# Two one-word mask tiles moved, so that every small SBUF tile starts 64 bytes lower

## The chip, the core and the metric

The kernel runs on one core of one Trainium2 chip. The metric is the device time of one execution, in microseconds (us); the lower the better. A core has a tensor engine (PE, with its weight loads shown apart as PEld), a vector engine (DVE), a scalar engine (ACT), GpSimd (POOL) and a queue engine that issues the DMAs (SP). They share one on-chip memory, SBUF, of 128 partitions. A tile is a piece of it that begins at the same byte in every partition.

## What is computed

Two linear layers with low-rank adapters, each added to its own input. `x` is 8 x 256 x 1024 in float32, every weight matrix is 1024 x 1024, and the adapter of each batch is chosen by an index:

```
def layer0(x, label, W, A, Bw):          # rank 32, 3 adapters in use
    return einsum('bsi,oi->bso', x, W) + 0.5 * einsum('bsr,or->bso', einsum('bsi,bir->bsr', x, A[label]), Bw)

def layer1(x, slot, W, b, As, Bs):       # rank 16, 24 adapters in use
    return einsum('bti,oi->bto', x, W) + b + 2 * einsum('btr,bro->bto', einsum('bti,bir->btr', x, As[slot]), Bs[slot])

x = x + layer0(x, itok_B_0_2, L0_cond_W, L0_cond_lora_A, L0_cond_lora_B_w)
x = x + layer1(x, itok_B_0_23, L1_cond_W, L1_cond_b, L1_cond_lora_As, L1_cond_lora_Bs)
```

## The kernel before

The kernel first forms the product of (1 + W0) and (1 + W1) and then applies it to every batch, so that the large part of both layers is one matrix product per batch. Each float32 operand is split into a high and a low part (`_hi`, `_lo`, the type fp32r), and a product is three matmuls: high by high, high by low, low by high. Both the product of the weights and that of each batch follow a scheme of seven half-size products (names `s1` to `s4`, `t1` to `t4`, `v11`, `vt2` and so on are the sums it needs).

**Stages.** Up to about 116 us the weights are loaded, turned and multiplied; the adapters of all batches are folded into small matrices in between (`q_step` and `c_step`, from 23 to 62 us and from 84 to 90 us). Then come eight batches of about 22.7 us; six of them run in a loop. On PE a batch is: seven products of 12 matmuls with 512 columns (`product`), eight matmuls of the input with the adapter matrix (`u_product`), one small correction (`corr`), and the low-rank parts (`low_rank`, `low_rank_rest`). The order on every engine is written out by hand, and semaphores tie the engines together.

**Names in the profile.** A matmul row reads `bank<-moving,stationary`: the first name is the operand that streams through the array (here with 512, 256 or 128 columns), the second is the one that was loaded as weights by the LDWEIGHTS before it. `by_halves`, `row_product`, `vm1_high` and `product` take both operands from large tiles. `q_step` takes its weights from `b0_st`, `c_step` from `a1_st` or `a1d_hi`/`a1d_lo`, `u_product` from `ac`, `low_rank` from `u_st` (its moving operand is `p_hi`), `corr` from `b0a1` (moving `u_st`), and `low_rank_rest` moves `e_p`. The digits of the names are left out in part: `a_st`, `b_st`, `b0a`.

**The map of SBUF.** All tiles have offsets written out by hand. 23 large slots of 8192 bytes per partition (`SLOT`) lie first; the large tiles, made by `big` and a few others, are in them. Behind them lie `eye` and `blank` (512 bytes each), then `MASKS` (64 bytes, with `bias_mask` at 0 and `low_mask` at 32, one float each), and then all the other small tiles in a row: `index` at `INDEX`, `b0a1` and `b0a1_all` at `B0A1`, the tiles at `U` (`u_st`, `u_sum`, `q`, `u_part`), `p_hi`, `e_raw` and `e_p` at `P_LO`, `b1_raw`, `a1d` and `hh` at `B1_RAW`, `b0_st`, `ac` and `e_hi` at `B0_ST`, `b0_raw` and `a0_raw`, `ct`, `a1_raw`, `m1_sum`, `u2_sum` and `z_sum` at `CT`, and `a1_st`, `c_hi` and `c_lo` at `C`. Every one of these sizes except `MASKS` is a multiple of 128 bytes. The common base of all offsets, the start of free SBUF rounded up to 32, is byte 1152 in this program, 9 times 128. So the large tiles, `eye` and `blank` begin at multiples of 128, and everything from `INDEX` on begins 64 bytes past one.

Of the kernel before, what the change touches and what calls it, by code (L numbers as in the profile page):

```python
# [5 lines left out]
F32 = mybir.dt.float32  # L6
# [5 lines left out]
P = 128  # L12
# [7 lines left out]
def two_layer_lora_kernel(nc, x, label0, slot1, w0, a0, b0w, w1, bias, a1, b1, out):  # L20
# [13 lines left out]
    SLOT = HK * H * 4  # L34
    EYE = 23 * SLOT
    BLANK = EYE + P * 4
    MASKS = BLANK + P * 4
    INDEX = MASKS + 64
    B0A1 = INDEX + 256
    U = B0A1 + 1024  # L40
    P_HI = U + 3 * S * 4
# [7 lines left out]
    def at(name, shape, dt, offset):  # L49
        size = 4  # L50
        for n in shape[1:]:
            size *= n
        assert base + offset + size <= nc.sbuf_usable_end, name
        return nc.alloc_sbuf_tensor_at(name, shape, dt, offset=base + offset)
# [53 lines left out]
    blank = at("blank", [P, P], F32R, BLANK)  # L108
    index = at("index", [1, 2 * B], I32, INDEX)
    index_f = at("index_f", [1, 2 * B], F32, INDEX + 64)  # L110
    index_wrap = at("index_wrap", [1, 2 * B], F32, INDEX + 128)
    index_ok = at("index_ok", [1, 2 * B], I32, INDEX + 192)

# [28 lines left out]
    e_p = at("e_p", [P, H], F32R, P_LO + H * 4)  # L142
    e_hi = at("e_hi", [P, H], F32R, B0_ST + KT * P * 4)

    bias_mask = at("bias_mask", [P, 1], F32, MASKS)
    low_mask = at("low_mask", [P, 1], F32, MASKS + 32)
    u_part = at("u_part", [64, S], F32, U + 2 * S * 4)
    p_hi = at("p_hi", [P, D], F32R, P_HI)
    b1_raw = at("b1_raw", [P, D], F32, B1_RAW)
# [1438 lines left out]
```

## Time and profile before

| | us |
|---|---|
| median of 3 runs | 297.86 |
| lowest and highest of them | 296.70 and 298.05 |
| the profiled execution | 299.37 |
| its span, first to last instruction | 297.6 |
| PE busy | 293.0 |
| DVE busy | 242.2 |
| ACT busy | 153.2 |
| POOL busy | 29.6 |

A matmul's row has its start and its duration; matmuls overlap in the array, and so the time that one costs the engine is the distance from its start to the start of the next, its pace, and not its duration. Starts are given to 0.01 us, so a pace is best read over a stretch of many matmuls: the difference of two starts divided by the number of matmuls between them.

### The profile page before, as it was taken

How to read it: one execution, taken by the hardware profiler on the slowest of the kernel's cores; microseconds unless marked ns; L12 is line 12 of the kernel's file. 1: busy time of each engine (PE TensorE's matmuls, PEld its weight loads, DVE VectorE, ACT ScalarE, POOL GpSimd, SP SyncE). 2: the span in 40 equal slices, each digit the busy share in tenths (PEclk: the TensorE clock that was granted, in tenths of full speed). 3: DMA queues.
4: the chain of work that ended last, by engine and by line, in shares of the span. 5: the costliest groups of instructions: out<-in, count | busy, mean ns of one | idle time of the engine just before them, and what ended most of it. 6: DMA issues, size and time to landing. Idle time of an engine off the chain costs nothing.

```text
span 297.6 us, 4449 instructions
## 1 busy us (share of the span) xinstructions
PE 293.0 (98%) x1334; PEld 238.0 (80%) x1334; DVE 242.2 (81%) x368; ACT 153.2 (51%) x270; POOL 29.6 (10%) x81
## 2 busy tenths in 40 slices
PE   7999999999999999999999999999999999999996
PEld 6888888888888888877878878878878878887875
DVE  3499996999999999899997797698698698696442
ACT  3376466879355737266374364365355355355120
POOL 1717100010000501100100100100100100100000
PEclk9999999999999999999999999999999999999999
DMA  6999620620003710065168068058158149013003
GB/s 181 322 281 343 77 34 1 108 36 2 0 0 72 124 35 1 0 110 174 26 108 222 4 107 224 0 101 216 17 105 213 18 85 240 10 35 142 0 1 143
DMA packets 100803, 29.17 MB, mean 98 GB/s; under 512 B 85548, under 2 KB 93996, under 8 KB 100788
## 3 DMA queue, kind: packets, MB, share of 16 engines
q1 hardware_dynamic: 100788, 28.99, 42.1%
q8 instruction: 7, 0.11, 0.1%
q14 instruction: 8, 0.07, 0.1%
HBM read 20.59 MB, written 8.39 MB: 97 GB/s over the span
## 4 chain that ended last, share of the span: by engine, by line
PE 97%; DMA 1%; DVE 0%; SPq 0%; issue 0%
PE bank L1196 93%; PE bank L1219 2%; DMA a<-in_L_cond_W 1%; PE bank L1438 1%; PE bank L1405 0%; SPq L274 0%; DVE a_hi L757 0%; DVE y L717 0%; DVE a L717 0%
## 5 line engine op out<-in xcount | busy, mean ns | idle before, releaser
L1196 PE MATMUL bank<-v_hi,lhs 128*128 128x512 f32 (+1 forms) x136 | 42.6, 378 | 0.0
L1196 PE MATMUL bank<-vt_hi,s_lo 128*128 128x512 f32 x96 | 37.5, 390 | 0.0
L1196 PE MATMUL bank<-vt_lo,s_hi 128*128 128x512 f32 x96 | 37.4, 390 | 0.0
L1196 PE MATMUL bank<-vt_hi,s_hi 128*128 128x512 f32 x96 | 37.4, 390 | 0.0
L964 DVE STREAM_TRANSPOSE xt<-raw 128x512 int32<-128x512 int32 x32 | 32.5, 1082 | 0.1
L1196 PEld LDWEIGHTS bank<-v_hi,lhs 128*128 128x128 f32 x136 | 25.1, 188 | 5.1 <-issue 0.4
L470 ACT ACTIVATE lhs<-xt 128x512 fp32r<-128x512 f32 x32 | 19.6, 625 | 12.6 <-PE bank L1196 12.3
L1196 PE MATMUL bank<-v_lo,lhs 128*128 128x512 f32 (+1 forms) x68 | 25.8, 380 | 0.0
L1196 PE MATMUL bank<-vt_hi,lhs 128*128 128x512 f32 x64 | 22.0, 404 | 0.0
L717 DVE TENSOR_TENSOR lhs<-xt,lhs 128x512 fp32r<-128x512 f32 x32 | 21.7, 684 | 0.3
L717 DVE TENSOR_TENSOR s_lo<-s_sum,s_hi 128x512 fp32r<-128x512 f32 x32 | 21.1, 682 | 0.2 <-ACT s_hi L470 0.2
L1196 PEld LDWEIGHTS bank<-vt_hi,s_hi 128*128 128x128 f32 x96 | 18.0, 188 | 3.9
L1196 PEld LDWEIGHTS bank<-vt_lo,s_hi 128*128 128x128 f32 x96 | 18.0, 188 | 3.9
L1196 PEld LDWEIGHTS bank<-vt_hi,s_lo 128*128 128x128 f32 x96 | 18.0, 188 | 3.8
L436 POOL CAST ac<-c_hi 128x128 fp32r (+1 forms) x16 | 7.1, 446 | 136.9 <-PE bank L1196 100.2
L470 ACT ACTIVATE s_hi<-s_sum 128x512 fp32r<-128x512 f32 x32 | 19.1, 624 | 2.4 <-DVE s_sum L717 2.2
L1196 PE MATMUL bank<-t_hi,s_hi 128*128 128x512 f32 x48 | 19.1, 397 | 0.0
L1196 PE MATMUL bank<-t_hi,s_lo 128*128 128x512 f32 x48 | 18.8, 391 | 0.0
L1196 PE MATMUL bank<-t_lo,s_hi 128*128 128x512 f32 x48 | 18.7, 390 | 0.0
L470 ACT ACTIVATE u_part<-bank 64x256 f32<-64x256 f32 x8 | 3.0, 380 | 29.7 <-PE bank L1196 29.7
L717 DVE TENSOR_TENSOR y<-bank,u_sum 128x512 f32<-128x512 f32 x16 | 10.9, 683 | 7.1 <-PE bank L1196 7.1
L1196 PE MATMUL bank<-lhs,ac 128*128 128x512 f32 x64 | 16.2, 395 | 0.0
(170 smaller groups left out, 660.1 us busy)
## 6 DMA issues: line engine op xcount, KB each, us to landing
raw<-in_x SPq DMA_DIRECT2D x32, 256.0 KB, 5.0
out<-y SPq DMA_DIRECT2D x31, 256.0 KB, 2.8
n<-in_L_cond_W SPq DMA_DIRECT2D x16, 256.0 KB, 5.7
a<-in_L_cond_W SPq DMA_DIRECT2D x16, 256.0 KB, 5.5
a_raw<-in_L_cond_lora_A SPq DMA_DIRECT2D x8, 128.0 KB, 2.5
b_raw<-in_L_cond_lora_Bs SPq DMA_DIRECT2D x16, 64.0 KB, 2.1
e_raw<-in_L_cond_lora_Bs SPq DMA_DIRECT2D x32, 32.0 KB, 1.8
a_raw<-in_L_cond_lora_As SPq DMA_DIRECT2D x8, 64.0 KB, 2.7
```

The source lines that it names most:

```text
L436: nc.gpsimd.tensor_copy(ac[:, :, at_col:at_col + R1], c_hi[:, :, cols].bitcast(F32)).then_inc(ac_c_made, 1)
L470: nc.scalar.activation(out_ap, in_ap, COPY, scale=scale).then_inc(made, 1)
L717: nc.vector.tensor_tensor(out_ap, one, other, op).then_inc(made, 1)
L964: nc.vector.transpose(xt[:, n, :, :].rearrange("p e (s sb) -> p sb e s", sb=GR).bitcast(I32), rows[:, n // 2, n % 2].bitcast(I32)).then_in ...
L1196: return nc.tensor.matmul(ps, lhsT, rhs, start=start, stop=stop, skip_group_check=more)
L1219: last = nc.tensor.transpose(ps[:, P * t:P * t + P], tile[:, j, t, :], eye[:, :])
L1438: return nc.tensor.matmul(ps, e_st[rows, P * t:P * t + P], e_p[rows, cols], start=False, stop=True, skip_group_check=True, tile_position=( ...
```

## The change

The 64 bytes of `MASKS` are taken away, so `INDEX` and all that lies behind it start 64 bytes lower, at multiples of 128. The two masks go to the free bytes behind `b0a1` and `b0a1_all` (which fill bytes 0 to 767 of the 1024 at `B0A1`), at 768 and 800. The instructions on every engine, their order and their waits are the same as before; only addresses differ.

```
-    MASKS = BLANK + P * 4
-    INDEX = MASKS + 64
+    INDEX = BLANK + P * 4
     B0A1 = INDEX + 256
     U = B0A1 + 1024
...
-    bias_mask = at("bias_mask", [P, 1], F32, MASKS)
-    low_mask = at("low_mask", [P, 1], F32, MASKS + 32)
+    bias_mask = at("bias_mask", [P, 1], F32, B0A1 + 768)
+    low_mask = at("low_mask", [P, 1], F32, B0A1 + 800)
```

## Rows read from the trace of the kernel before

**Rows 1.** The page: the span, and an engine's busy time, share and instructions.

```profile
span 297.6 us, 4449 instructions
PE 293.0 (98%) x1334; PEld 238.0 (80%) x1334; DVE 242.2 (81%) x368; ACT 153.2 (51%) x270; POOL 29.6 (10%) x81
```

**Rows 2.** The chain that ended last, by engine; PE's waits: total us, times, longest.

```profile
PE 97%; DMA 1%; DVE 0%; SPq 0%; issue 0%
...
PE bank L1196 <- DVE a_hi L757: 0.6, 1, 0.6
```

**Rows 3.** One turn of the loop by engine: length, busy us (instructions), PEclk, DMA, GB/s.

```profile
177.43:200.16 22.73, 22.73 (x105) 18.20 (x105) 18.43 (x30) 10.99 (x21) 1.34 (x6) 1.00 0.47 106
```

**Rows 4.** Groups of matmuls: names, shapes, count, then busy us and mean ns.

```profile
L1196 PE MATMUL bank<-b_hi,s_hi 128*128 128x512 f32 x16 | 6.2, 389 | 0.0
...
L1196 PE MATMUL bank<-a_hi,a_st 128*128 128x512 f32 x16 | 5.2, 396 | 0.0
```

**Rows 5.** Timeline of PE before the batches: start us, us, names, shapes.

```profile
51.85 0.40 PE L1196 MATMUL bank<-a_hi,a_st 128*128 128x512 f32 x1
...
57.45 1.11 PE L1196 MATMUL bank<-a_st,b_st 128*128 128x256 f32 x8
58.40 0.40 PE L1196 MATMUL bank<-t_hi,b_st 128*128 128x512 f32 x1
...
62.14 0.40 PE L1196 MATMUL bank<-b_hi,a_hi 128*128 128x512 f32 x1
...
63.76 0.39 PE L1196 MATMUL bank<-b_lo,a_hi 128*128 128x512 f32 x1
...
73.05 0.39 PE L1196 MATMUL bank<-b_hi,s_hi 128*128 128x512 f32 x1
...
83.93 0.40 PE L1196 MATMUL bank<-s_hi,a_st 128*128 128x512 f32 x1
```

**Rows 6.** Timeline of PE in a turn of the loop, 163.6 to 176.6 us.

```profile
163.61 2.03 PE L1196 MATMUL bank<-lhs,ac 128*128 128x512 f32 x8
165.47 0.39 PE L1196 MATMUL bank<-vt_hi,s_hi 128*128 128x512 f32 x1
...
166.86 0.39 PE L1196 MATMUL bank<-vt_hi,s_hi 128*128 128x512 f32 x1
...
170.94 0.39 PE L1196 MATMUL bank<-v_hi,lhs 128*128 128x512 f32 x1
...
171.28 0.40 PE L1196 MATMUL bank<-v_lo,lhs 128*128 128x512 f32 x1
...
172.91 0.62 PE L1196 MATMUL bank<-v_hi,lhs 128*128 128x512 f32 x2
...
173.81 0.62 PE L1196 MATMUL bank<-p_hi,u_st 128*128 128x512 f32 x2
174.27 0.40 PE L1196 MATMUL bank<-v_hi,s_hi 128*128 128x512 f32 x1
...
176.59 0.39 PE L1196 MATMUL bank<-v_lo,s_hi 128*128 128x512 f32 x1
```

**Rows 7.** Timeline of PE at the end: matmuls with 256 columns, all from large tiles.

```profile
291.88 0.27 PE L1196 MATMUL bank<-v_lo,lhs 128*128 128x256 f32 x1
...
294.50 0.28 PE L1196 MATMUL bank<-v_hi,lhs 128*128 128x256 f32 x1
```

**Rows 8.** Groups on ACT: a bank copied to a small tile, and to a large one.

```profile
L470 ACT ACTIVATE m_sum<-bank 128x512 f32<-128x512 f32 x8 | 4.8, 599 | 2.3 <-PE bank L1196 1.8 <-DVE y L717 0.5
...
L470 ACT ACTIVATE m<-bank 128x512 f32<-128x512 f32 x8 | 4.3, 608 | 1.5 <-PE bank L1196 1.5
```

**Rows 9.** Timeline of DVE beside rows 6.

```profile
168.50 0.75 DVE L1019 SCALAR_TENSOR_TENSOR e_p<-e_hi,bias_mask,e_raw 128x512 fp32r<-128x512 f32 x1
...
169.78 0.68 DVE L717 TENSOR_TENSOR s_sum<-xt 128x512 f32<-128x512 f32 x1
```

## The prediction

> **What bounds the kernel now.** I read the page's busy times first, then the chain of work that ended last and PE's waits, then the loop by engine, then PE's timeline. PE is busy for 293.0 of 297.6 us [rows 1]; the chain that ended last is PE for 97% of the span, and the wait shown is 0.6 us and lies in the weight stage's first microseconds [rows 2]. One turn of the loop takes 22.73 us and PE is busy in all of it, with a granted clock of 1.00, the upper of its two levels, while DVE is busy for 18.43 us and ACT for 10.99 [rows 3]. So the kernel lasts as long as PE's list of matmuls takes, and a change that moves no instruction can matter only by the pace of these matmuls, or by making another engine so slow that PE has to wait. DVE has 4.3 us of room in a turn, ACT 11.7.
>
> The pace isn't the same everywhere. From 73.05 to 83.93 us PE runs 48 matmuls of 512 columns whose operands both lie in large tiles: 10.88 / 48 = 226.7 ns each. From 51.85 to 57.45 us it runs the 24 of `c_step`, in the same pattern of three and into one bank of the accumulator: 5.60 / 24 = 233.3 ns each [rows 5]. The only thing in the code that sets them apart is where the weights come from: `a1_st`, a small tile that begins 64 bytes past a multiple of 128, and not a large one. The group means say the same: 389 ns for weights from a large tile, 396 for weights from `a_st` [rows 4]. In the loop it recurs. `u_product` (weights from `ac`) runs from 163.61 to 165.47: 1.86 / 8 = 232.5 ns. The next six matmuls, large tiles again, still take 1.39 / 6 = 231.7, and then 18 run from 166.86 to 170.94 at 4.08 / 18 = 226.7 [rows 6]. So there seems to be a quick pace and a slow one about 6.7 ns longer; weights from a tile 64 bytes off bring the slow one, and it takes some matmuls with aligned weights to return.
>
> **The change, part by part.** Taking `MASKS` out moves every tile from `INDEX` on down by 64 bytes, to multiples of 128. Nothing is added or removed on any engine, queue or semaphore, so there are no instructions to price; what is priced is the pace of the matmuls that load weights from the moved tiles.
>
> Before the batches these are 32 with `b0_st` at 512 columns (8 + 8 for the first half of `q`, 16 for the second), 36 with `a1_st` and 12 with `a1d_hi` or `a1d_lo`, 80 in all. 80 x 6.7 ns = 0.53 us. Behind two of these stretches the pace has to recover: from 62.14 to 63.76 us seven matmuls take 1.62 where 7 x 226.7 = 1.59 [rows 5], 0.03 us, and I give the second, at the end of the `c_step` of 84 to 90 us, the same. Sum 0.59 us.
>
> In each batch: `u_product`, 1.86 - 8 x 0.2267 = 0.05 us; its recovery, 1.39 - 6 x 0.2267 = 0.03 us; two `low_rank` with weights from `u_st`, 173.81 to 174.27, 0.46 - 0.453 = 0.01 us, and the ten matmuls behind them, 174.27 to 176.59, 2.32 - 2.267 = 0.05 us [rows 6]. Sum 0.14 us, and eight batches give 1.1 us. I take the third `low_rank`, which runs alone, and `low_rank_rest`, whose weights `e_st` lie in a large slot, at nothing. Behind `corr` seven matmuls run from 171.28 to 172.91, 1.63 - 1.587 = 0.04 us over [rows 6]; `corr` is short as well as off alignment, and a short matmul leaves less time to hide the next weight load. So this is between 0 and 8 x 0.04 = 0.3 us, and I take 0, since its shortness stays.
>
> The matmuls with 256 columns give nothing: eight with both operands from small tiles take 58.40 - 57.45 = 0.95 us, 119 ns each [rows 5]; aligned ones take 294.50 - 291.88 = 2.62 for 22, also 119 ns [rows 7]. That is a warning too: an unaligned weight load isn't dearer in itself there, and I can't say by what the 512-column ones get slower.
>
> The other engines write and read the moved tiles as well. An ACT copy of a bank takes 599 ns into the small `m1_sum` and 608 into the large `m1` [rows 8], so I take that at nothing, and either sign of such 9 ns is covered by the room of ACT and DVE. Loads into moved tiles end at other addresses; no DMA stands among PE's waits [rows 2], so a load that is some ns faster or slower is hidden. The masks are written once by POOL and read as a column by DVE; their place costs nothing. If the cover failed, it would take 4.3 us of added DVE work in a turn before PE waited.
>
> The sum: 0.59 + 1.1 = 1.7 us less, up to 2.0 with `corr`. Every such ns is on the chain that sets the end. The profiled execution would go from 299.37 to 297.7 us; its own time is 1.5 above the median, and so the median goes from 297.86 to **296.2 us**, 0.57% less.
>
> **A page's rule against it.** The rows show a slower pace for a tile 64 bytes off [rows 4, 5]. The Trainium skill, on the page "SBUF — State Buffer", section "Specifications (TRN2)", gives SBUF cachelines of 16 bytes, and its section "Operand start alignment" asks only for a multiple of the element size, while saying that it speaks of legality and that nothing was timed. By these a shift of 64 bytes leaves every operand's line-up as it was and the sum would be 0, not 1.7 us; this is the rival "no change" below. The trace so far disagrees about the pace, but not yet about the cause.
>
> **The rivals.**
> *No change.* All tiles that are 64 bytes off are also the last ones in SBUF, behind the large slots, and nothing in the profile parts the two: no aligned small tile is used as weights at 512 columns. If the slow pace belongs to the region, or to something that these matmuls share beside their address, it stays. The 256-column rows, equal at 119 ns, speak a little for that [rows 5, 7]; against it, `c_step` and `row_product` have the same shape and pattern. 297.9 us. The change would not do what it says, too, if the base weren't a multiple of 128; it is byte 1152, so I give this next to nothing.
>
> *Half of it.* The moved weights run at the quick pace, but the slow stretches behind them in the batches have another reason, such as the waits that stand there in the code. Then the gain is 0.53 + 8 x 0.05 = 0.9 us: 296.9 us, within 0.5%.
>
> *Slower.* What PE dislikes may be other engines' accesses at the same place within 128 bytes as its own. Today the small tiles that DVE and ACT write for much of a turn stand 64 bytes apart from PE's large ones; aligned, they would meet. Should half of the 105 matmuls of a turn fall to the slow pace by that, 52 x 6.7 ns x 8 = 2.8 us would be added, and without any gain the time is 300.7 us. It decides from 250 slowed matmuls on (1.7 us / 6.7 ns), where it eats the gain. Against it: from 166.86 to 170.94 PE holds 226.7 ns [rows 6] while DVE writes `e_p`, a small tile, and then `s_sum`, an aligned large one [rows 9]; neither disturbed it.
>
> **How the numbers follow.** The full gain gets 0.56, half of it 0.15, no change 0.21, slower 0.08. A measurement of this kernel can tell about 0.5% from no change, 1.5 us. The full gain of 1.7 to 2.0 us is barely over that, and the three runs of before lie 1.35 us apart, so I give it 0.8 to come out as faster: with a little from the half case, faster is 0.48. Slower is 0.08, and the rest, 0.44, is no change that can be told. The range starts at 295.2, the upper end of the gain (2.0 us) and 0.6 for the scatter of the median, and ends at 298.3, no change with 0.4 for scatter; this leaves out the slower case and the tails.
>
> **What would show it.** In the profile after: the 24 matmuls of `c_step` at 226.7 ns and their group mean at 389 instead of 396; `lhs,ac` likewise, with the next product quick from its first matmul; the product behind the two `low_rank` at 226.7; a turn of the loop at 22.6 us instead of 22.73; the 256-column rows, DVE, ACT and the DMAs as before. If `c_step` still takes 233 ns, alignment isn't the cause and the forecast falls. If `c_step` is quick but a turn is shorter by only 0.05 us, it is the half case. If large-tile matmuls leave 226.7 in stretches that were quick, it is the slower one.

## The result

The changed kernel takes 295.46 us (median of 4 runs, 295.17 to 295.81), the kernel before 297.83 (4 runs, 296.70 to 298.05): a ratio of 0.9928, 95% interval 0.9901 to 0.9956. Two further comparisons on other occasions, told below, gave 0.9948 (0.9930 to 0.9965) and 0.9944 (0.9923 to 0.9966). So the change makes the kernel faster by about half a per cent.

The profile after, in the views of before. First the page (busy us, share, instructions); it answers to [rows 1]:

```profile
span 294.1 us, 4449 instructions
PE 289.8 (99%) x1334; PEld 236.4 (80%) x1334; DVE 242.8 (83%) x368; ACT 153.4 (52%) x270; POOL 30.6 (10%) x81
```

The groups of matmuls, mean ns last but one. `a_st` had 396 and, from large tiles, `b_hi,s_hi` 389 [rows 4]:

```profile
L1195 PE MATMUL bank<-lhs,ac 128*128 128x512 f32 x64 | 15.8, 389 | 0.0
...
L1195 PE MATMUL bank<-a_hi,a_st 128*128 128x512 f32 x16 | 5.1, 389 | 0.0
```

The timeline of PE (start us, us, names, shapes), for `c_step` and for one turn of the loop; it answers to [rows 5, 6]:

```profile
49.47 0.39 PE L1195 MATMUL bank<-a_hi,a_st 128*128 128x512 f32 x1
...
54.91 1.12 PE L1195 MATMUL bank<-a_st,b_st 128*128 128x256 f32 x8
...
160.63 1.98 PE L1195 MATMUL bank<-lhs,ac 128*128 128x512 f32 x8
162.44 0.39 PE L1195 MATMUL bank<-vt_hi,s_hi 128*128 128x512 f32 x1
...
163.80 0.39 PE L1195 MATMUL bank<-vt_hi,s_hi 128*128 128x512 f32 x1
...
168.23 0.40 PE L1195 MATMUL bank<-v_lo,lhs 128*128 128x512 f32 x1
...
170.78 0.62 PE L1195 MATMUL bank<-p_hi,u_st 128*128 128x512 f32 x2
171.24 0.39 PE L1195 MATMUL bank<-v_hi,s_hi 128*128 128x512 f32 x1
...
173.50 0.39 PE L1195 MATMUL bank<-v_lo,s_hi 128*128 128x512 f32 x1
```

The 24 matmuls of `c_step` take 5.44 us, 226.7 ns each, where they took 233.3. `u_product` takes 1.81 us instead of 1.86, the six behind it 1.36 instead of 1.39, and the ten behind the two `low_rank` 2.26 instead of 2.32. So these places with weights from small tiles now run at the pace of the large ones.

**Where the time went.** The two profiled spans differ by 3.5 us, more than the medians (2.37), because their first 20 us differ. The first matmul of `q_step` in the kernel before, and then the same and the last matmul of all in the changed one:

```profile
23.61 0.40 PE L1196 MATMUL bank<-b_hi,b_st 128*128 128x512 f32 x1
```
```profile
21.32 0.39 PE L1195 MATMUL bank<-b_hi,b_st 128*128 128x512 f32 x1
...
290.94 0.28 PE L1195 MATMUL bank<-v_hi,lhs 128*128 128x256 f32 x1
```

The last matmul of before starts at 294.50 [rows 7]. That is 270.89 against 269.62 us: **1.27 us come from the pace**, 0.43%. Of this, 0.56 us lies between `q_step` and the first `u_product` (which starts at 117.66 and 114.81 us, so 94.05 against 93.49 us) and 0.71 in the batches. The rest of the difference between these two profiles, 2.3 us, lies ahead of `q_step`.

### The profile page after: what moved, and what is told of

Read it like the earlier page. It is cut to its first block, busy times and chain, and to the rows that moved or that the text cites. A ratio compares the mean times of both kernels' runs of the same rounds, so it can differ in the third digit from the quotient of the medians.

```text
span 294.1 us, 4449 instructions
## 1 busy us (share of the span) xinstructions
PE 289.8 (99%) x1334; PEld 236.4 (80%) x1334; DVE 242.8 (83%) x368; ACT 153.4 (52%) x270; POOL 30.6 (10%) x81
## 4 chain that ended last, share of the span: by engine, by line
PE 97%; DMA 1%; DVE 0%; SPq 0%; issue 0%
PE bank L1195 93%; PE bank L1218 2%; DMA a<-in_L_cond_W 1%; PE bank L1437 1%; PE bank L1404 0%; SPq L273 0%; DVE a_hi L756 0%; DVE y L716 0%; DVE a L716 0%
## 5 line engine op out<-in xcount | busy, mean ns | idle before, releaser
L469 ACT ACTIVATE vt_hi<-vt 128x512 fp32r<-128x512 f32 x16 | 10.1, 631 | 11.0 <-DVE vt L716 10.5
```

Of the source, the lines that this page charges most:

```text
L469: nc.scalar.activation(out_ap, in_ap, COPY, scale=scale).then_inc(made, 1)
```

## The experiments

### Is the rest of the gain the change's?

Two kernels as they are, for more timings and more profiles.

> The kernel before, as it is, for a second profile of its first 20 us and of its pace. If the clock's rise belongs to the execution, the first matmuls of 512 columns may as well be quick here (few at 427 ns), and the time from the first q_step matmul to the end is 271.1 us as in the first profile. If the rise belongs to the change, this profile shows eight matmuls at 427 ns again. Ratio 1.000.

> The changed kernel once more. Its first profile is 3.5 us shorter than that of before: 1.3 us of it lies in the pace of the matmuls (counted row by row), 2.3 us in the first 20 us, where the granted clock rose some 3 us earlier. Theory: the early rise belongs to the execution and not to the change, so over more executions the median falls by 1.3 us plus whatever the chances of the clock give: ratio 0.993 to 0.997. Rival: the change itself brings the clock up earlier, and every execution of it gains 3 us or more: ratio 0.988 to 0.990. In both the 24 matmuls of c_step with weights from a1_st take 226.7 ns.

Measured: the kernel before against itself 0.9999 (0.9987 to 1.0012); the changed kernel 295.53 against 296.92 us, ratio 0.9948 (0.9930 to 0.9965). The second profile of the kernel before, first matmuls with 512 columns and then the two ends used above:

```profile
5.71 1.20 PE L1196 MATMUL bank<-b_hi,a_hi 128*128 128x512 f32 x4
6.74 1.07 PE L1196 MATMUL bank<-b_lo,a_hi 128*128 128x512 f32 x4
...
20.82 0.40 PE L1196 MATMUL bank<-b_hi,b_st 128*128 128x512 f32 x1
...
291.73 0.28 PE L1196 MATMUL bank<-v_hi,lhs 128*128 128x256 f32 x1
```

The first profile of before had, in the same place:

```profile
6.44 2.05 PE L1196 MATMUL bank<-b_hi,a_hi 128*128 128x512 f32 x4 [0.64 <-DVE a_hi L757]
8.29 1.48 PE L1196 MATMUL bank<-b_lo,a_hi 128*128 128x512 f32 x3
```

(The second row counts only three because the window that it was read in ends there.)
### Absolute place or distance?

In the first experiment all tiles, large and small, lie 64 bytes off; in the second the large ones alone. "Distance" means from here on how many bytes behind the large tiles' place a small tile begins, counted within 256: it is 64 before the change and 0 after it.

```
all_off:
-    base = (nc.sbuf_base + 31) // 32 * 32
+    base = (nc.sbuf_base + 31) // 32 * 32 + 64
large_off, that line and:
-    INDEX = BLANK + P * 4
+    INDEX = BLANK + P * 4 + 64
-    U = B0A1 + 1024
+    U = B0A1 + 896
```

> The changed kernel with the common base 64 bytes higher: every tile, large and small, begins 64 bytes past a multiple of 128. Theory of the absolute address: every weight load at 512 columns is now off, some 1150 matmuls of 512 columns at 233.3 instead of 226.7 ns, +7 us or more against the changed kernel, about 303 us, ratio to the kernel before 1.018 to 1.025. Rival, the relative place: slow only where weights and moving operand differ within 128 bytes; here none do, and the time is that of the changed kernel, ratio 0.993.

> Large tiles 64 bytes off, small tiles aligned (the 128 unused bytes behind b0a1_all make the room). Theory of the absolute address: matmuls with weights from large tiles at 233.3 ns, those with weights from ac, b0_st and a1_st (moving operand from a large tile that is off) at 226.7 ns; about 302 us, ratio 1.014 to 1.022. Rival, the relative place: the other way round, ac, b0_st and a1_st slow and all else quick, as in the kernel before, ratio 1.000.

Measured: `all_off` 295.77 us, 0.9963 (0.9947 to 0.9980); `large_off` 295.92, 0.9968 (0.9954 to 0.9983). `c_step` in `all_off`, and then, in `large_off`, `c_step`, the eleven matmuls behind `corr`, and `u_product`:

```profile
49.25 0.39 PE L1195 MATMUL bank<-a_hi,a_st 128*128 128x512 f32 x1
...
54.69 1.11 PE L1195 MATMUL bank<-a_st,b_st 128*128 128x256 f32 x8
```
```profile
49.53 0.39 PE L1195 MATMUL bank<-a_hi,a_st 128*128 128x512 f32 x1
...
55.02 1.12 PE L1195 MATMUL bank<-a_st,b_st 128*128 128x256 f32 x8
...
145.82 0.39 PE L1195 MATMUL bank<-v_lo,lhs 128*128 128x512 f32 x1
...
148.32 0.62 PE L1195 MATMUL bank<-p_hi,u_st 128*128 128x512 f32 x2
...
160.88 2.00 PE L1195 MATMUL bank<-lhs,ac 128*128 128x512 f32 x8
162.71 0.40 PE L1195 MATMUL bank<-vt_hi,s_hi 128*128 128x512 f32 x1
```

With every tile off alignment, `c_step` takes 5.44 us, as quick as when every tile was aligned, and a turn of the loop takes 22.63 us, as in the changed kernel. The theory of the absolute address, with its 303 us, has fallen: my own reading, "weights from a tile that isn't aligned", was wrong. With the small tiles at multiples of 128 and the large ones off, `c_step` takes 5.49 us, 228.8 ns each, and `u_product` 1.83: slower than the changed kernel, as the rival says, but not by as much as before; the ratio of 1.000 that I had written for it was missed too, at 0.9968. Here I had overlooked something: the 128 bytes that I took out for room put the small tiles at a distance of 192 from the large ones, where they stood at 64 before. So 64 and 192 differ, and a pattern of 128 bytes can't hold both.

### How often does the pattern repeat?

```
small_128:
-    U = B0A1 + 1024
+    U = B0A1 + 896
off_32_96:
-    B0_ST = B1_RAW + D * 4
+    B0_ST = B1_RAW + D * 4 + 32
-    C = CT + 3 * H * 4
+    C = CT + 3 * H * 4 + 64
off_160_224: all three lines
```

> The changed kernel with U and all tiles behind it 128 bytes lower (an unused 128 bytes behind b0a1_all is taken out), so they stand 128 bytes off from the large tiles within 256, as they stand at 0 in the changed kernel. The runs so far: distance 64 gives 233.3 ns, distance 192 gives 229.0, distance 0 gives 226.7 whatever the absolute place. If what counts repeats every 128 bytes, all matmuls stay at 226.7 and a turn of the loop at 22.63 us. If it repeats only every 256 bytes or more, 128 is as far off as can be and ac, b0_st and a1_st run slower, at 229 ns or above, a turn at 22.68 or more.

> The changed kernel with b0_st and ac (and the tiles around them) 32 bytes up from a multiple of 128 and a1_st (with c_hi and c_lo) 96 bytes up; u_st, p_hi and the a1d tiles stay aligned. By the distance theory only the matmuls with weights from b0_st, ac and a1_st change: a penalty that grows with the distance gives ac and b0_st about 230 ns and a1_st about 237; one that asks only whether the place is the same gives both 233.3. If only 64-byte distances matter, both stay at 226.7. In all cases a1d_hi and the low_rank pair stay at 226.7.

> As small_128, with b0_st and ac another 32 bytes up (distance 160) and a1_st another 96 up (distance 224). If the pattern repeats every 128 bytes, they run as at 32 and 96 in the run beside it. If it repeats every 256, distance 224 lies nearest to 192 and 0 and gives 227 to 229 ns, and 160 between that of 128 and that of 192.

These had one execution with a profile each: 296.59, 296.73 and 298.00 us, beside 298.83 for the kernel before. With starts that differ as told above, such single times decide nothing, and the paces are what is read. `c_step` in `small_128`, with two `u_product` five turns apart:

```profile
49.24 0.39 PE L1195 MATMUL bank<-a_hi,a_st 128*128 128x512 f32 x1
...
54.81 1.12 PE L1195 MATMUL bank<-a_st,b_st 128*128 128x256 f32 x8
...
138.17 2.02 PE L1195 MATMUL bank<-lhs,ac 128*128 128x512 f32 x8
...
251.77 2.02 PE L1195 MATMUL bank<-lhs,ac 128*128 128x512 f32 x8
```

This kernel has all small tiles at multiples of 128, exactly what the change is said to be for, and yet `c_step` takes 5.57 us, 232.1 ns each, and a turn (251.77 - 138.17) / 5 = 22.72 us, as before the change. `off_32_96`, `c_step`, the end of the eight matmuls with 256 columns behind it, and `u_product`, and then `off_160_224`, `c_step` and an earlier `u_product`:

```profile
49.55 0.40 PE L1195 MATMUL bank<-a_hi,a_st 128*128 128x512 f32 x1
...
55.16 1.11 PE L1195 MATMUL bank<-a_st,b_st 128*128 128x256 f32 x8
56.11 0.39 PE L1195 MATMUL bank<-t_hi,b_st 128*128 128x512 f32 x1
...
161.19 2.02 PE L1195 MATMUL bank<-lhs,ac 128*128 128x512 f32 x8
163.06 0.39 PE L1195 MATMUL bank<-vt_hi,s_hi 128*128 128x512 f32 x1
```
```profile
50.34 0.40 PE L1195 MATMUL bank<-a_hi,a_st 128*128 128x512 f32 x1
...
55.94 1.11 PE L1195 MATMUL bank<-a_st,b_st 128*128 128x256 f32 x8
...
139.39 2.02 PE L1195 MATMUL bank<-lhs,ac 128*128 128x512 f32 x8
141.25 0.40 PE L1195 MATMUL bank<-vt_hi,s_hi 128*128 128x512 f32 x1
```

Together, by the distance of the weights' tile from the large tiles, within 256 bytes:

| distance | stretch | ns per matmul |
|---|---|---|
| 0 | `c_step`, changed kernel and `all_off` | 226.7 |
| 32 | `u_product`, `off_32_96` (1.87 / 8) | 233.8 |
| 64 | `c_step`, before | 233.3 |
| 96 | `c_step`, `off_32_96` (5.61 / 24) | 233.8 |
| 128 | `c_step`, `small_128` | 232.1 |
| 160 | `u_product`, `off_160_224` (1.86 / 8) | 232.5 |
| 192 | `c_step`, `large_off` | 228.8 |
| 224 | `c_step`, `off_160_224` (5.60 / 24) | 233.3 |

A stretch of eight is read to a little over 1 ns, one of 24 to 0.5. Apart from 192 the cost is there or it isn't; it doesn't grow with the distance, as one of the theories for `off_32_96` had it, and my expectation that 224 would be near to the quick end was wrong. Distance 192 is dear by only 2 ns, which I can't explain; in that kernel the large tiles lie elsewhere than in most others, but in `all_off` they lie there too, and it is quick. In the changed kernel the tiles at `U` and behind lie 256 bytes past the large ones within 512, and they are quick: 256 counts as 0.

The 256-column matmuls are a case of their own. The eight of [rows 5] take both operands from small tiles, which stand at the same place as each other, so they couldn't show the cost. In `off_32_96` their two tiles are 64 bytes apart (`a1_st` at 96, `b0_st` at 32), and they take (56.11 - 55.16) / 8 = 0.119 us all the same.

### Which stretch got dearer by the change?

In the batches the kernel gained less than its quick places promise. Two candidates: `e_p`, which is only a moving operand, and `u_st`, which is both. (The lines that give the two masks a free place are left out below.)

```
ep_off_64:
-    U = B0A1 + 1024
+    U = B0A1 + 768
-    P_LO = P_HI + D * 4
-    B1_RAW = P_LO + D * 4
+    P_LO = P_HI + D * 4 + 64
+    B1_RAW = P_LO + D * 4 + 192
u_off_64:
-    U = B0A1 + 1024
-    P_HI = U + 3 * S * 4
+    U = B0A1 + 768 + 64
+    P_HI = U + 3 * S * 4 + 192
```

> The changed kernel with only e_raw and e_p 64 bytes off (distance 64, as in the kernel before); the masks lie in the gap behind them. e_p is only ever a moving operand. In the changed kernel the 14 matmuls from the last low_rank_rest to the end of the next product of vt take 3.51 and 3.55 us in turns, in the kernel before 3.51. Theory: what counts is the distance between a moving operand and the weights that are loaded while it streams, so e_p's place sets the recovery behind it: here 3.51 us in every batch and a turn of the loop 0.02 us shorter (22.61). Rival: only the place of the weights counts, and nothing changes: 3.51 and 3.55 in turns, 22.63 us.

> The changed kernel with only the tiles at U (u_st, u_sum, u_part) 64 bytes off, ac, b0_st, a1_st, b0a1, p_hi and e_p aligned. u_st is the moving operand of corr and the weights of low_rank. By the theory of distance u_product stays at 226.7 ns and the rest goes back to what it was before: the eleven matmuls behind corr take 2.53 us instead of 2.56, the ten behind the two low_rank 2.32 instead of 2.27, a turn of the loop about 22.65 to 22.68 instead of 22.63. Rival, that recovery behind corr and low_rank hangs on b0a1 and p_hi: 2.56, 2.27 and 22.63 us as in the changed kernel.

These two had one execution each as well (294.98 and 295.81 us, beside 297.35 for the kernel before). From `low_rank_rest` to the `low_rank` at the end of the next product, in two turns of the changed kernel, and then in `ep_off_64`, with its `u_product` five turns apart:

```profile
151.63 0.50 PE L1437 MATMUL bank<-e_p,e_st 32*128 32x512 f32 x4
...
154.96 0.39 PE L1195 MATMUL bank<-p_hi,u_st 128*128 128x512 f32 x1
...
174.27 0.51 PE L1437 MATMUL bank<-e_p,e_st 32*128 32x512 f32 x4
...
177.57 0.39 PE L1195 MATMUL bank<-p_hi,u_st 128*128 128x512 f32 x1
```
```profile
137.30 1.98 PE L1195 MATMUL bank<-lhs,ac 128*128 128x512 f32 x8
...
150.95 0.50 PE L1437 MATMUL bank<-e_p,e_st 32*128 32x512 f32 x4
...
154.23 0.39 PE L1195 MATMUL bank<-p_hi,u_st 128*128 128x512 f32 x1
...
250.28 1.98 PE L1195 MATMUL bank<-lhs,ac 128*128 128x512 f32 x8
```

The changed kernel takes 3.33 and 3.30 us in turns. With `e_p` back at distance 64 it is 3.28, as in the kernel before (154.64 to 157.92 us there), and a turn takes (250.28 - 137.30) / 5 = 22.60 us. So a moving operand's place matters too, and at this place distance 64 is better than 0. That `e_p` moved along cost the change some 0.03 us a turn. The edit isn't quite pure: it also puts the tiles at `U` and `P_HI` 256 bytes lower, so that they meet the large ones within 512. No run has that shift alone; against its having a part, the eleven matmuls behind `corr`, which moves `u_st`, take the same in this kernel as in the changed one, to 0.01 us.

In `u_off_64`, from the matmul behind `corr` to the two `low_rank`, and on to the eleventh matmul behind them:

```profile
145.18 0.40 PE L1195 MATMUL bank<-v_lo,lhs 128*128 128x512 f32 x1
...
147.71 0.63 PE L1195 MATMUL bank<-p_hi,u_st 128*128 128x512 f32 x2
148.17 0.39 PE L1195 MATMUL bank<-v_hi,s_hi 128*128 128x512 f32 x1
...
150.47 0.39 PE L1195 MATMUL bank<-v_lo,s_hi 128*128 128x512 f32 x1
```

Behind `corr` eleven matmuls take 2.53 us; in the changed kernel it is 170.78 - 168.23 = 2.55, in the kernel before 173.81 - 171.28 = 2.53 [rows 6]. The ten behind the two `low_rank` take 2.30 us, against 2.26 changed and 2.32 before. Both went the way that `u_st`'s place said, with `b0a1` and `p_hi` left where they were, so the rival has fallen, though 2.30 isn't all of 2.32. Its turn, from two `u_product` starts at 137.58 and 250.97, is 22.68 us.

`large_off` has one more value for `u_st`, at distance 192: there the eleven matmuls behind `corr` take 148.32 - 145.82 = 2.50 us, hardly more than 11 x 226.7 ns = 2.49. `corr` is the same short matmul in all kernels, so the slow stretch behind it doesn't come from its shortness alone; it goes with the place of `u_st`, and distance 0 is the dearest of those seen here (2.55 at 0, 2.53 at 64, 2.50 at 192; in `large_off` the weights `b0a1` lie elsewhere too, at 64, but between 64 in the kernel before and 0 in `u_off_64` their place made no difference: 2.53 us in both).

### A kernel with the better of both

`ep_off_64` is the best by its profile. It was timed beside the changed kernel.

> The changed kernel with e_raw and e_p 64 bytes off, now timed. Its one profile has a turn of the loop at 22.596 us, against 22.627 of the changed kernel and 22.723 of the kernel before, and 1.41 us less than the kernel before from the first matmul of q_step to the last one. If the pace is all that differs, the ratio to the kernel before is 0.9952, with the start of each execution as scatter: 0.9935 to 0.9970. The same profile again: turn 22.60 us.

> The changed kernel beside it on the same chip. By pace alone 1.27 us less than the kernel before, ratio 0.9957, within 0.994 to 0.9975, and 0.13 to 0.2 us above the kernel with e_p moved, which the scatter of single executions will hide. If its ratio is nearer to the first comparison's 0.993, the start of the execution has a part in the gain. The turn is 22.63 us.

Measured: 295.56 us, ratio to the kernel before 0.9933 (0.9913 to 0.9953), and for the changed kernel 295.71, 0.9944 (0.9923 to 0.9966). The turn was 22.60 and 22.63 us again. The gain of 0.13 us by pace is the same in two profiles and can't be told in the timings.

## Why the prediction was right, and where it wasn't

**What bounds the kernel.** Right: the time went down by what PE's matmuls gave up, and no engine made PE wait in exchange; DVE and ACT are busy for 242.8 and 153.4 us, against 242.2 and 153.2 before.

**The setup's term** (80 matmuls at 6.7 ns and two recoveries, 0.59 us). Right: `c_step` gave back 5.60 - 5.44 = 0.16 us, which is 24 x 6.7 ns, and the whole stretch from `q_step` to the first `u_product` gave back 0.56 us.

**The batches' term** (0.14 us each, 1.1 in all). Too large: 0.71 us came. A turn went from (254.50 - 140.89) / 5 = 22.72 us to (251.12 - 137.99) / 5 = 22.63, by the starts of `u_product` in the two traces:

```profile
140.89 2.03 PE L1196 MATMUL bank<-lhs,ac 128*128 128x512 f32 x8
...
254.50 2.03 PE L1196 MATMUL bank<-lhs,ac 128*128 128x512 f32 x8
```
```profile
137.99 1.98 PE L1195 MATMUL bank<-lhs,ac 128*128 128x512 f32 x8
...
251.12 1.98 PE L1195 MATMUL bank<-lhs,ac 128*128 128x512 f32 x8
```

The four places that I counted did give what I counted. The step that failed is the one that set `corr` and `low_rank_rest` at "nothing": the recovery behind `corr` became 0.02 to 0.03 us longer, not shorter, and the one behind `low_rank_rest`, whose moving `e_p` I didn't consider, by about as much in the mean of two turns. I had bounded `corr` at 0 to 0.3 us of gain and excluded a loss without a reason, and I had put its slow stretch down to its shortness, which `large_off` contradicts (2.50 us with the same short matmul). The third `low_rank`, also put at nothing, gave back a little: with the three matmuls behind it, it takes 0.91 us where it took 0.92.

**The sum.** 1.7 us forecast, 1.27 measured by pace. The median of 295.46 us lies near the lower end of the range, 295.2 to 298.3, and 0.7 below the forecast of 296.2; by pace alone it would have been 297.83 - 1.27 = 296.6, above the forecast. So the first comparison's 2.37 us flatters the forecast by luck: the profiles show differences of that size in the start of single executions. The three comparisons gave 2.37, 1.39 and 1.78 us.

**The cause.** "A tile 64 bytes past a multiple of 128" was the wrong description. The rival "no change", that alignment isn't what counts, was right in its premise and wrong in its result: what counts for `c_step`, `q_step` and `u_product` is whether the small tiles stand at the same place as the large ones within 256 bytes, and that the change brings them there is luck. `small_128` is what that rival described: small tiles at multiples of 128, and the slow pace. The page that I cited ("SBUF — State Buffer" of the Trainium skill, "Specifications (TRN2)" and "Operand start alignment") speaks of 16-byte lines and of legality. What I drew from it, that 64 bytes change nothing, disagrees with `c_step` at 233.3 and 226.7 ns.

**The half rival** fell with the six matmuls behind `u_product`, which are quick from the first one on (1.36 us). **The slower rival** was refuted as forecast: in `all_off` and in the changed kernel everything that DVE and ACT write lies at PE's place, and PE holds 226.7 ns.

**What stays open.** No run was made to tell whether the partner of a weight load is the moving operand of its own matmul or that of the one before. The kernel before speaks against the first alone: `p_hi` and `u_st` stand at the same place there, and still the ten matmuls behind the two `low_rank` take 2.32 us [rows 6]. By what the address acts on the pace isn't shown by any run. Nor is it known why the pace needs up to eleven matmuls to recover, why distance 192 costs less, or why `e_p` and `u_st` as moving operands do better apart.

## What to carry to other kernels

Where PE bounds a kernel and loads new weights for every 512-column matmul, compare the distance between starts, group by group: 389 against 396 ns in the means of two groups gave this away. In long stretches of such matmuls, weights and moving operands whose addresses are equal within 256 bytes gave the quick pace here; alignment to 128 alone didn't help, and a common shift of everything did no harm. For a single odd matmul between them (`corr`, `low_rank_rest`) the equal place wasn't the best one, so each place is to be measured. Judge such a change by the distance between two fixed matmuls in the traces, which repeated to 0.04 us, and not by the span, in which the first 20 us alone moved by 2.8 us in the same kernel.

## What the runs showed of the hardware

- The pace of a 512-column matmul with a fresh weight load is 226.7 ns, or 232 to 234 ns where the two tiles don't lie at the same place within 256 bytes (228.8 at distance 192). With 256 columns no such difference shows: 119 ns with the two tiles 64 bytes apart (`off_32_96`) and 119 with both in large tiles [rows 7].
- After a disturbance (a short matmul, weights from another place) the pace takes some matmuls to come back: 6 behind `u_product` and about 10 behind `low_rank` before the change [rows 6], none behind either after it. Behind `corr` eleven take between 2.50 and 2.55 us, by the place of `u_st`.
- The first 512-column matmuls ran at 427 or at about 227 ns from one execution of the same kernel to the next. The record of the granted clock's upper level begins at 10.91 us in the one and at 5.59 in the other, though the profile's views show 1.00 throughout in both.
